# Query reloads issued by SyncE instead of ScalarE, and rope buffers in another order, in an attention and mixture-of-experts kernel

## What is computed

```python
q = jnp.einsum('bim,ghmd->bghid', x, w_aq)
k = jnp.einsum('bim,gmd->bgid', x, w_ak)
v = jnp.einsum('bim,gmd->bgid', x, w_av)
q = _rope(q)
k = _rope(k)
s = jnp.einsum('bghid,bgjd->bghij', q * qk_mult, k * qk_mult)
s = s - jnp.asarray(INF_APPROX, dtype=s.dtype) * mask        # causal
p = jax.nn.softmax(s, axis=-1)
o = jnp.einsum('bghij,bgjd->bghid', p, v)
r = jnp.einsum('bghid,ghdm->bim', o, w_ao)
...
x = _layernorm(x + attention(x)); x = _layernorm(x + experts(x))
```

## Time and profile before

| | |
|---|---|
| median of 3 runs | 1074.1 us (1068.6 to 1076.94) |
| the profiled execution | 1073.27 us, its span 1071.5 us |
| granted TensorE clock, mean | 0.957 of full |
| PE busy | 965.9 us |
| DVE busy | 681.1 us |
| ACT busy | 488.6 us |
| POOL busy | 371.8 us |

### The profile page before, as it was taken

How to read it: one execution, slowest core, us unless ns; L and a number is a source line. 1 busy time by engine, 2 the same in 40 slices (tenths; PEclk the granted TensorE clock), 3 DMA queues, 4 the chain that set the end, 5 groups by cost and what they waited for, 6 DMA issues and landing times.

```text
span 1071.5 us, 16751 instructions
## 1 busy us (share of the span) xinstructions
PE 965.9 (90%) x5240; PEld 739.3 (69%) x5240; DVE 681.1 (64%) x1703; ACT 488.6 (46%) x1083; POOL 371.8 (35%) x334
## 2 busy tenths in 40 slices
PE   8999979989999999999979999999999998559745
PEld 6888867667787778776767667888787776336412
DVE  5989853775766675757565668575857666424326
ACT  4012124555656564645544456564645544125402
POOL 4878863234323121021244332312031112126811
PEclk9999988999999999999979999999999999769968
DMA  8696765463222111111243224351112133978687
GB/s 254 228 289 218 250 230 159 127 165 110 73 64 61 60 52 58 45 33 50 85 133 90 84 74 132 87 156 45 56 31 69 44 79 99 274 214 194 86 279 284
DMA packets 137303, 137.24 MB, mean 128 GB/s; under 512 B 18065, under 2 KB 108805, under 8 KB 137216
## 3 DMA queue, kind: packets, MB, share of 16 engines
q1 hardware_dynamic: 84064, 98.33, 30.1%
q10 hardware_dynamic: 43872, 29.50, 9.4%
q0 software_dynamic: 9280, 8.34, 4.5%
HBM read 86.44 MB, written 63.05 MB: 140 GB/s over the span
## 4 chain that ended last, share of the span: by engine, by line
PE 67%; DVE 10%; issue 8%; SPq 5%; DMA 5%; ACT 2%; POOL 2%; ACTq 1%; DVEq 0%; POOLq 0%
PE s_ps L1116 14%; PE ring L1126 9%; PE o_ps L1146 8%; PE o_ps L1143 8%; PE ring L1155 7%; PE s_ps L1095 6%; PE ring L1095 5%; DVE neg_max L1319 2%; SPq L759 2%; PE s_ps L1209 2%; PE o_ps L1095 2%; SPq L655 1%; PE s_ps L1119 1%; DVE pt_lo L1253 1%; DMA inverses<-inv_t 1%
## 5 line engine op out<-in xcount | busy, mean ns | idle before, releaser
L1319 DVE TENSOR_REDUCE neg_max<-s_ps 128x1 f32<-128x128 f32 (+7 forms) x256 | 191.6, 750 | 137.6 <-PE s_ps L1119 131.8
L961 ACT ACTIVATE probs<-s_ps,neg_max 128x128 f32<-128x128 f32 (+7 forms) x256 | 189.7, 741 | 142.3 <-DVE neg_max L1319 127.8
L1116 PE MATMUL s_ps<-kt,qt_hi 128*128 128x512 f32 (+3 forms) x768 | 235.2, 388 | 6.0 <-ACT probs L961 3.9
L824 POOL TENSOR_TENSOR qt_lo<-q_raw,qt_hi 128x512 fp32r<-128x512 f32 x64 | 82.1, 1283 | 319.3 <-ACT qt_hi L875 319.0
L1126 PE MATMUL ring<-ident,probs 128*128 128x128 f32 x1152 | 177.5, 277 | 9.2 <-DVE pt_lo L1253 5.1
L875 ACT ACTIVATE pt_hi<-ring 128x512 fp32r<-128x512 f32 x168 | 99.8, 596 | 181.8 <-PE ring L1126 173.6
L1116 PEld LDWEIGHTS s_ps<-kt,qt_hi 128*128 128x128 f32 x768 | 139.7, 194 | 54.9 <-issue 30.2
L1253 DVE TENSOR_TENSOR pt_lo<-ring,pt_hi 128x512 fp32r<-128x512 f32 x168 | 115.4, 687 | 62.2 <-ACT pt_hi L875 56.7
L1126 PEld LDWEIGHTS ring<-ident,probs 128*128 128x128 f32 x1152 | 129.1, 142 | 33.7 <-issue 14.5
L1146 PE MATMUL o_ps<-pt_hi,v 128*128 128x512 f32 x336 | 145.9, 435 | 1.4 <-DVE pt_lo L1253 0.9
L1116 PE MATMUL s_ps<-kt,qt_lo 128*128 128x512 f32 (+3 forms) x384 | 134.6, 350 | 0.0
(11 more groups left out here) (201 smaller groups left out, 1378.8 us busy)
## 6 DMA issues: line engine op xcount, KB each, us to landing
qk_rows<-prods SPq DMA_DIRECT2D x80, 256.0 KB, 2.8
q_raw<-qk_rows ACTq DMA_DIRECT2D x128, 128.0 KB
inv_row<-inverses SPq DMA_DIRECT2D x64, 256.0 KB
fsum<-sums SPq DMA_DIRECT2D x48, 256.0 KB, 8.1
sums<-blank SPq DMA_DIRECT2D x16, 640.0 KB
wexp<-in_L_ffn_w_gate_dram SPq DMA_DIRECT2D x32, 192.0 KB, 5.0
wexp<-in_L_ffn_w_up_dram SPq DMA_DIRECT2D x32, 192.0 KB, 5.2
wexp<-in_L_ffn_w_down_dram SPq DMA_DIRECT2D x32, 192.0 KB, 6.3
```

The source lines that it names most:

```text
L961: act.activation(probs[:, u % 2, h, 0:blocks(u) * P], s_ps[:, n % 2, score_cols(n)], ACT.Exp, bias=neg_max[:, n % 8:n % 8 + 1], accum_out= ...
L1116: pe.matmul(s_ps[:, n % 2, c + a:c + e], q[qp], k[kp][:, a:e], start=(qp == kp == 0), stop=(qp == 1 and not last))
L1319: dve.tensor_reduce(neg_max[:, n % 8:n % 8 + 1], s_ps[:, n % 2, score_cols(n)], AX_X, ALU.max, negate=True).then_inc(max_ready, 1)
```

## The change

Two things are changed. First, `load_q` is issued by SyncE. The places in SEQ and the conditions are the same, but SyncE now passes them in its own order, in which the rope stores, the V stores and the inverses stand. Second, the three rope buffers are numbered differently: the one that shares memory with kt1 is now number 0, which holds the last pair, and the other two, which share memory with pt and its neighbours, are numbers 1 and 2. The first eviction waits for the stores of sets 1 and 2 alone.

```diff
-        prods = [sb("prods2", [P, 2, 2, CW], F32, raw)]
+        prods = [sb("prods0", [P, 2, 2, CW], F32, raw)]
...
-        prods = [sb(f"prods{n}", [P, 2, 2, CW], F32, pre) for n in range(2)] + prods
+        prods += [sb(f"prods{n}", [P, 2, 2, CW], F32, pre) for n in (1, 2)]
...
+            def load_q(u):
+
+                i, g = divmod(u, G)
+                rope_done(sp, i // CHUNK, g)
+                for z in range(2):
+                    src = rows_of[1 + g, z, :, i * P:(i + 1) * P].rearrange("(h d) t -> d h t", h=H)
+                    sp.dma_start(q_raw[z * D // 2:(z + 1) * D // 2, u % QB, :].rearrange("d (h t) -> d h t", h=H), src
+                                  ).then_inc(q_loaded[u % QB], 16)
+
...
+                if s == ("proj", CHUNKS - 1, 1, 0, 0):
+                    sp.wait_ge(proj_ready, PROJ_AT[("proj", CHUNKS - 1, 0, 1, 1)] + 1)
+                    for u in range(QB):
+                        load_q(u)
+                if s[0] == "qsplit" and 1 <= s[1] < UNITS - 2:
+                    sp.wait_ge(q_ready, s[1])
+                    load_q(s[1] + 2)
...
-                if s == ("proj", CHUNKS - 1, 1, 0, 0):
-                    act.wait_ge(proj_ready, PROJ_AT[("proj", CHUNKS - 1, 0, 1, 1)] + 1)
-                    for u in range(QB):
-                        load_q(u)
...
-                    if 1 <= u < UNITS - 2:
-                        act.wait_ge(q_ready, u)
-                        load_q(u + 2)
...
-                        rope_done(act, CHUNKS - 1, 3)
+                        for k in range(2, 2 * SETS):
+                            act.wait_ge(rope_stored[k], 16 * len(range(k // 2, len(ROPE_AT), SETS)))
```

More of the change, by code:

```diff
@@ L875, in split @@
                 return act.activation(hi, raw, ACT.Copy)
[L877 to L884, removed]
             for s in SEQ:
```

## The result

| | before | changed |
|---|---|---|
| median of 12 runs each | 1076.1 us (1068.6 to 1082.6) | 1082.4 us (1075.8 to 1086.1) |
| profiled execution (span) | 1073.3 (1071.5) | 1082.4 (1080.6) |
| TensorE, ScalarE busy | 90%, 46% | 89%, 45% |

The ratio is 1.0062, with a 95% interval of 1.0032 to 1.0091, or +6.7 us. Both lie within 1% of the kernel before. They hold the +4.2 of the sum, but not for the reasons that the sum gave.

The account below looks back on a forecast made before the run. TensorE was 90% busy, but SyncE's round trip of softmax inverses was taken to set tile 0's pace. Terms +4.4 − 0.7 + 1.2 − 0.7 = +4.2 us gave 1078 us, range 1069 to 1084.

Parts of the forecast that it names:

- edit 1, first eviction: Start of attention: the first eviction goes some 3 us earlier, priced at nothing because SyncE's chain does not contain it.
- edit 2, ScalarE's relief: Attention: taking 64 loads off ScalarE's queue gains 0.7 us, between nothing and 11, since little was held up.
- edit 3, loads before the stage change: Last rope pairs: load_q(0) to (2) behind pair 33's stores delay query splits 1 to 3 us, hidden, priced at nothing.
- edit 3, three loads ahead of inverses: Tile 0: load_q(4) to (6) ahead of the inverses of units 0 to 2 add three times 1.47, +4.4 us.
- v_rows store: Store at 155.03: its 1.65 us issue may collide with ScalarE's q load; moving that away gives −0.7 us.
- later tiles: From tile 1 on: SyncE has slack waiting for VectorE, so its added loads are priced at nothing.
- clock: Tile 0's output projection: after longer TensorE idling, part of it runs at half clock, +1.2 us.
- one for one: Last rope pair: beyond 4.4 us of slip, it and all behind it would be late by the same amount.
- the waits shrink: Rival, tile 0: inverse-write waits fall from 3.8 us, paying back the added issue; 1070 to 1072 us, chance 0.22.
- The small writes queue behind the loads: Rival, tile 0: three units' inverse writes wait 1.2 us more each, +3.6 us; 1081 to 1088 us, chance 0.18.
- ScalarE's relief: Rival, whole attention: exps come earlier, gaining 5 to 11 us while SyncE hides its part; 1062 to 1068 us, chance 0.07.
- the first sign: Profile after: the last rope pair moving from 152 us would show the forecast wrong.

Follow-up runs that it names:

- e1: Against the kernel before, only the reordered prods buffers and the shorter first-eviction wait, with ScalarE issuing every q load; 1076.8 us, ratio 1.0016.
- e6: Against the changed kernel, load_q(0) to (6) left on ScalarE, the other 57 loads on SyncE; 1075.0 us, ratio to before 1.0003.
- r1: The changed kernel itself, timed and profiled a second time; 1080.8 us, ratio to before 1.0035.
- e2: Against the kernel before, only the q loads moved to SyncE, with the old buffers and the old eviction wait; 1080.9 us, ratio 1.0058.
- e9: Against the changed kernel, load_q(4) and later moved behind each unit's inverse writes, all loads still on SyncE; 1074.5 us, ratio to before 0.9997.
- e4: Against e3, SyncE's loads from load_q(4) on moved behind each unit's four inverse writes, ahead of the wait; 1071.9 us, ratio to before 0.9966.
- e8: Against r3, each transfer of load_q(0) to (2) cut into two of half the heads; 1082.4 us, ratio to before 1.0068.
- e5: Against e4, load_q(0) to (2) moved to SyncE where the changed kernel has them; 1075.3 us, ratio to before 0.9987.
- e3: Against the changed kernel, load_q(0) to (3) back on ScalarE, later loads on SyncE ahead of the inverse writes; 1078.1 us, ratio to before 1.0022.
- r2: e4 itself, timed again; 1072.5 us, ratio to before 0.9980.
- r3: e5 itself, timed again; 1073.2 us, ratio to before 0.9981.
- e7: Against e4, the four loads of the output weights wo issued together with the first one; 1075.7 us, ratio to before 1.0005.

## Why the prediction was right in its sum and wrong in its parts

Measured is the change in the profiled executions, up to the end of tile 0's output projection, where the whole difference of 7.3 us had arisen.

| term | predicted | measured |
|---|---|---|
| edit 1, first eviction | 0 | 0 (e1) |
| late before the first q load | | +1.8, scatter |
| edit 2, ScalarE's relief | −0.7 | none seen; e6 cannot resolve 0.7 |
| edit 3, loads before the stage change | 0 | +2.6 |
| edit 3, three loads ahead of inverses | +4.4 | +4.4 issue, +0.6 writes, −1.3 waits, −1.3 read-back |
| v_rows store | −0.7 | −1.2 |
| later tiles | 0 | none seen (e6) |
| clock | +1.2 | +1.6 |
| sum | +4.2 | +7.3 (terms rounded) |

Without the scatter the change cost 5.5 us in this execution. That the sum came out near is in part luck: the loads before the stage change were missed by 2.6 us, and tile 0 was overpriced by 2.5 (+3.7 for its two terms, where +1.2 was measured; r1 has +2.6).

**The step that failed** is "That hides in GpSimd's 4.38 us of idle time before the last pair … Price nothing". It cost 2.6 us in the profiled execution, 2.8 in r1, 3.3 in e2, and 2.6 us between the medians of e9 and e4. The idle time of the earlier trace rows is still there:
```profile
156.59 2.51 POOL L830 TENSOR_TENSOR prods<-prods 128x512 f32<-128x512 f32 x2 [4.39 <-DVE prods L1307]
```
It could not be used up, since it is a wait for VectorE, which waits for TensorE, which computes one pair after another. The delay took another way: SyncE's stores release the prods buffers, VectorE fills them, and TensorE's banks are free only when VectorE has read them. The cover that mattered was the slack of the stores against VectorE, and I read it nowhere. The price was a branch of my own sum, beyond 4.4 us late "one for one", but with the wrong threshold. I also counted load_q(3) nowhere; what it adds stays open.

**Three loads ahead of the inverses.** Their issue was priced rightly. Between the end of a read's issue and the next writes lie 1.54 and 1.59 us (167.31 to 168.85, 173.64 to 175.23), where the earlier trace rows have 0.05 (161.98 to 162.03). The period is 6.3 us, not the 6.5 to 7 foreseen, since the waits did not keep their 3.8 us: in the chain the three writes' landings are 3.71, 3.23 and 3.23 us against 3.36, 4.13 and 4.00 in the earlier trace rows, and the read-back is 3.45 against 4.76. From the last pair to the third multiply the whole came to +1.2 us in place of +3.7. In r1 the waits shrank less (landings of 3.80, 3.89 and 3.64 us), the period was 7.0 and 6.8 us, and the whole +2.6. That is part of the rival "the waits shrink", which was given 0.22; it took back 2.6 us but not the 4.4 that it needed. e4 shows what the term hid: the position, not the queue, is what costs. Behind the writes no cost of the same loads can be seen, and the distance is 1.8 to 3.0 us under that of the kernel before. Part of that is not the loads' place: e1 and e6, whose SyncE issues no q load before the third unit's read-back, are already 1.3 and 1.0 us under it.

**The small writes queue behind the loads** did not come true. The Trainium skill ("DMA: Bandwidth & Descriptors", Queues, rings and completion order) says that descriptors of one queue are taken in ring order, which I had turned into 1.2 us more for each wait; the landings of the second and third unit's writes came 0.9 and 0.8 us sooner, and only the first unit's 0.35 us later. Before the stage change rows speak both ways. The second store behind the loads landed after 6.38 us in e8 but after 3.00 in e5, with the same 768 KB of loads ahead of it. The fourth landed after 5.94, 6.22, 6.30 and 6.47 us (changed, r1, e9, e2), where stores ahead of the loads took 3.92 to 4.54 in the same chains; but that one has three stores of 256 KB ahead of it as well. So no run here bears the rule out or refutes it at that place.

**ScalarE's relief** did not show, as the gapless rows had suggested. The attention from the third multiply to hid took 758.0 us in the changed kernel, 761.2 in r1 and 756.4 before, with 754.3 to 758.3 in e1 to e6. So the 5 to 11 us of that rival are excluded, by e6's interval too (0.9977 to 1.0029); the 0.7 us of the sum are less than these executions can tell.

**The clock** was near the forecast. Windows of 1 us on TensorE's engine in the changed kernel: window, us, PE busy, PEclk, DMA share, GB/s:
```profile
182.00:183.00 1.00, 0.00 (x0) 1.00 0.77 223
...
184.00:185.00 1.00, 1.00 (x3) 0.71 0.00 0
185.00:186.00 1.00, 1.00 (x5) 0.50 0.39 129
...
187.00:188.00 1.00, 1.00 (x4) 0.58 0.83 249
```
TensorE idled 3.11 us before its "pv" at 183.95 and was then granted half rate, 1.2 GHz, from about 184.4 to 187.8. The three steps ahead of the projection took 3.20 us where they had taken 1.98, and the projection 7.30 against 6.91: 1.6 us together. In r1 and e3 the same pieces lost 2.9 us each.

**What would have shown it.** Three of the signs named in the prediction spoke against it at once. The last rope pair moved from 152, and the waits after the writes were shorter than 3.8 us. And q loads came too late; ScalarE's split of the first unit stood for them, 8.66 us ahead of 138.64, where it had stood 4.09 us ahead of 132.24 before. By the first sign, the absolute times fell due late as well: unit 0's writes began at 161.99 in place of 158.7, and the projection at 187.16 in place of 184.5. Others held: ScalarE's idle time before its first eviction was gone (158.96, no wait), all was late by one constant from 200 us on, and nothing was gained between 200 and 880. In r1 the constant did not hold as well: the end of the projection was 8.5 us late and the hid transpose 10.3.

**A version that beats the changed kernel, and perhaps the one before.** e4 measured 0.9966 and 0.9980 of the kernel before, and the two kernels with three loads more on SyncE 0.9987 and 0.9981: 1071.9 to 1075.3 us. The first interval, 0.9949 to 0.9984, leaves 1 out; the other three reach it, so a gain over the kernel before is shown in one comparison of four. Against the changed kernel r2 and r3 are 7.6 to 8.3 us faster on the same chip.

## What to carry to other kernels

An instruction moved to another in-order queue costs its issue time where the work behind it is on the path, and nothing that these runs could see inside a wait that stands there already: the same two transfers for each unit were worth 4 to 7 us more ahead of four small writes than behind them. Before an idle time is counted as cover, follow who ends it: GpSimd's 4.38 us could hide nothing, since it waited for the engine that came late. And where a queue releases buffers, read the slack between the release and its user, in several executions if the start scatters: here VectorE's wait went from 0 to 4 us as the loads were issued 0.3 to 2.1 us behind TensorE's step.

## What the runs showed of the hardware

- Issuing costs SyncE by the transfer and not by its bytes: 0.70 us each for six of 128 KB, 0.68 each for twelve of 64 KB.
- Four writes of 0.5 KB were waited for 1.6 us when hardly anything else moved (90 GB/s from 168 to 169 us, then none) and 5.8 us beside 2 MB of weights in one and the same kernel (e7).
- A SyncE transfer can take 1.2 us longer to issue just behind one of ScalarE's. The v_rows store of the earlier trace rows took 1.65 us, 0.22 us behind the end of ScalarE's q transfer. In e6, where ScalarE still issues that load, it took 1.64 us, 0.22 us behind it again. In the eleven kernels without a ScalarE load at this place it took 0.43 us. In e1, which has the load too, ScalarE's transfer ended 0.10 us after the store had begun, and the store took 0.43 us as well; so what exactly must meet is open.
